# Delta-rule attention block: dense products regrouped behind the small ones, the next rows' norm moved to ScalarE

## The reference

```
q, k = l2norm(xn Wq) * 32**-0.5, l2norm(xn Wk)     16 heads of 32
v, beta = silu(xn Wv), sigmoid(xn Wb)
S_t = S_(t-1) + k_t (beta_t (v_t - S_(t-1)^T k_t))^T;  o_t = S_t^T q_t
attention = (rmsnorm(o) * o_norm_weight) Wo
FFN = ((silu(xn Wg * sg) * (xn Wu * su)) Wd) * sd   1536 inner, weights rounded to fp8
```

## Time and profile before

| | us |
|---|---|
| median of 3 runs | 2276.19 (2276.04 to 2282.8) |
| the profiled execution | 2288.38 |
| its span, first to last instruction | 2286.6 |
| TensorE busy with products | 2122.0 (93%) |
| VectorE busy | 1947.2 (85%) |
| ScalarE busy | 987.0 (43%) |
| GpSimd busy | 267.4 (12%) |

### The profile page before, as it was taken

How to read it: one execution, slowest core, us unless ns; L and a number is a source line. 1 busy time by engine, 2 the same in 40 slices (tenths; PEclk the granted TensorE clock), 3 DMA queues, 4 the chain that set the end, 5 groups by cost and what they waited for, 6 DMA issues and landing times.

```text
span 2286.6 us, 82010 instructions
## 1 busy us (share of the span) xinstructions
PE 2122.0 (93%) x36464; PEld 1089.5 (48%) x36592; DVE 1947.2 (85%) x3591; ACT 987.0 (43%) x2525; POOL 267.4 (12%) x519
## 2 busy tenths in 40 slices
PE   2889999999999999999999999999999999999996
PEld 1445454554545455454544545445444444445453
DVE  8988989889898988888878888887888878898886
ACT  4652534435353443535335353342534425354442
POOL 2101011020101102011010101101011020110200
PEclk9999999999999999999999999999999999999998
DMA  7001111001111100111100111001111001111000
GB/s 262 20 3 21 38 21 39 17 7 39 21 38 21 39 12 12 39 21 38 21 11 30 21 38 21 29 12 21 38 22 39 7 16 38 21 38 22 11 12 20
DMA packets 89951, 68.47 MB, mean 30 GB/s; under 512 B 68480, under 2 KB 68480, under 8 KB 89600
## 3 DMA queue, kind: packets, MB, share of 16 engines
q1 hardware_dynamic: 88880, 63.20, 9.7%
q10 hardware_dynamic: 720, 0.03, 0.0%
HBM read 30.72 MB, written 16.78 MB: 21 GB/s over the span
## 4 chain that ended last, share of the span: by engine, by line
PE 84%; DVE 10%; issue 4%; DMA 1%; ACT 0%; SPq 0%; DVEq 0%
PE D L456 25%; PE D L446 23%; PE D L519 13%; PE T L371 12%; PE D L387 7%; PE T L363 4%; DVE state L1386 1%; DVE f_lo L1218 1%; DVE stats L917 1%; DMA qt<-in_L_attn_Wq_dram 1%; DVE outer_v L1232 1%; DVE outer_p L1382 1%; DVE at L1239 1%; DVE at L920 0%; DVE kq L1254 0%
## 5 line engine op out<-in xcount | busy, mean ns | idle before, releaser
L456 PE MATMUL D<-xt,wgu 128*128 128x512 f16 x3072 | 689.4, 380 | 15.9 <-ACT sg L739 6.7
L446 PE MATMUL D<-xt,w_hi 128*128 128x512 f16 x1664 | 493.5, 383 | 26.0 <-DVE w_lo L1004 24.1
L456 PEld LDWEIGHTS D<-xt,wgu 128*128 128x128 f16 x3072 | 291.0, 98 | 365.0 <-issue 10.6
L519 PE MATMUL D<-wd,f_hi 128*128 128x512 bf16 x752 | 286.1, 380 | 17.8 <-issue 15.4
L446 PE MATMUL D<-xt,w_lo 128*128 128x512 f16 x768 | 294.5, 384 | 0.2 <-issue 0.2
L1232 DVE TENSOR_TENSOR outer_v<-mt,at 128x62 f32<-128x62 f32 (+15 forms) x496 | 260.2, 525 | 13.6
L1239 DVE TENSOR_TENSOR at<-at,outer_v 128x62 f32<-128x62 f32 (+15 forms) x496 | 260.9, 526 | 11.8
L446 PEld LDWEIGHTS D<-xt,w_hi 128*128 128x128 f16 x1664 | 160.1, 99 | 217.7 <-issue 33.9
L794 ACT ACTIVATE qt<-T 64x128 f32<-64x128 f32 (+1 forms) x384 | 104.7, 273 | 355.9 <-DVE outer_p L1382 352.9
L519 PE MATMUL D<-wd,f_lo 128*128 128x512 bf16 x656 | 248.6, 379 | 0.8
L729 ACT ACTIVATE kpv<-kpv,rk 128x32 f32<-128x32 f32 x1024 | 231.1, 308 | 35.1 <-DVE kpv L1096 35.1
(11 more groups left out here) (175 smaller groups left out, 2783.1 us busy)
## 6 DMA issues: line engine op xcount, KB each, us to landing
xs<-_attn_hidden_states_dram SPq DMA_DIRECT2D x32, 512.0 KB, 3.4
out_dram<-xs SPq DMA_DIRECT2D x32, 512.0 KB, 3.0
fuse<-in_L_ffn_gate_w_dram SPq DMA_DIRECT2D x2, 768.0 KB, 9.0
xs<-in_L_ffn_up_w_dram SPq DMA_DIRECT2D x2, 768.0 KB, 9.0
f_hi<-in_L_ffn_down_w_dram SPq DMA_DIRECT2D x2, 768.0 KB, 10.4
f_lo<-in_L_ffn_down_w_dram SPq DMA_DIRECT2D x2, 768.0 KB, 12.0
kpv<-in_L_attn_Wk_dram SPq DMA_DIRECT2D x1, 1024.0 KB, 11.5
qt<-in_L_attn_Wq_dram SPq DMA_DIRECT2D x1, 1024.0 KB, 13.7
```

The lines of the kernel that those rows point to most:

```text
L446: last = nc.tensor.matmul(D[bank][:, :], w[:, k, cols], xp[:, k, :], start=n == 0, stop=n == len(products) - 1)
L456: last = nc.tensor.matmul(D[bank][:, :], wgu[:, n // 2, c:c + P], (xt_hi, xt_lo)[n % 2][:, n // 2, :], start=n == 0, stop=n == 2 * KT_ - 1)
L519: last = nc.tensor.matmul(D[bank][:, :], (f_hi, f_lo)[n % 2][:, ic, j * P:(j + 1) * P], wd[:, ic, :], start=n == 0, stop=n == 2 * IC - 1)
```

## The change

Four things are moved; the arithmetic stays.

1. `FILL_UW` goes from 8 to 12, and `FILL_CHAIN` from 7 to (5, 7). 48 + 96 = 144 dense products as before: all six gate and up jobs now end before the chunk steps, and each down job takes exactly two steps.
2. `grams_of(1)` comes four dense products later, inside `project(6)`.
3. The next rows' norm is applied by ScalarE as an activation with scale `rstd` and bias `shift`, where VectorE makes `shift` = -mean * rstd for two tiles at once. The four tiles are spread over steps 1 to 4.
4. What follows from 1 is re-ordered: `silu_gate(11)`, `fuse_tile(10)`, `fuse_tile(11)`, `low_part(9)`, `high_part(11)` earlier, the squares of the queries in steps 2, 3, 5 and 6.

```diff
-HIGH_AT, LOW_AT = {1: (0, 1), 3: (2, 3)}, {2: 0, 3: 1, 4: 2, 5: 3}
-SQUARE_AT = {3: (0, 1), 4: (2, 3)}
+HIGH_AT, LOW_AT = {1: (0,), 2: (1,), 3: (2,), 4: (3,)}, {2: 0, 3: 1, 4: 2, 5: 3}
+SQUARE_AT = {2: (0,), 3: (1,), 5: (2,), 6: (3,)}
-APPLY_LATE = {0: 0, 2: 1}
+SHIFT_AT = {0: 0, 1: 1}
-FILL_UW, FILL_CHAIN = 8, 7
+FILL_UW, FILL_CHAIN = 12, (5, 7)
     # fill_at
-    return 4 * FILL_UW + (2 * c + half) * FILL_CHAIN
+    return 4 * FILL_UW + c * sum(FILL_CHAIN) + half * FILL_CHAIN[0]
     # TensorE
                     project(5)
+                    project(6, end=4)
                     grams_of(1)
-                    project(6)
+                    project(6, first=4)
-                        fill(fill_at(c, 0), FILL_CHAIN)
+                        fill(fill_at(c, 0), FILL_CHAIN[0])
-                        fill(fill_at(c, 1), FILL_CHAIN)
+                        fill(fill_at(c, 1), FILL_CHAIN[1])
     # ScalarE, before and in the chunk steps
                     silu_gate(10)
+                    silu_gate(11)
                         if c == 0:
                             high_part(10)
-                        if c == 1:
-                            silu_gate(11)
-                        if c == 2:
                             high_part(11)
+                        for j in () if closing else HIGH_AT.get(c, ()):
+                            act.wait_ge(shift_ready, since(BATCH, j // 2 + 1))
+                            act.wait_ge(tt_ready, since(2, 2))
+                            nc.scalar.activation(xn[:, j], xs[:, 1 - par, j, :], ACT.Identity, bias=shift[:, j:j + 1], scale=rstd[:, j:j + 1]).then_inc(xn_ready, 1)
     # VectorE
-                    def apply_norm(b):
+                    def shift_of(b):
                         if closing:
                             return
+                        two = slice(2 * b, 2 * b + 2)
                         dve.wait_ge(rstd_ready, since(BATCH, b + 2))
-                        dve.wait_ge(tt_ready, since(2, 2))
-                        for j in (2 * b, 2 * b + 1):
-                            layer_norm_apply(j, 1 - par).then_inc(xn_ready, 1)
+                        nc.vector.scalar_tensor_tensor(shift[:, two], mv[:, two, 0], -1.0, rstd[:, two], ALU.mult, ALU.mult).then_inc(shift_ready, 1)
                     read_w(7)
+                    fuse_tile(10)
                     low_part(8)
                     aggregate(0)
                     aggregate(1)
                         if c == 0:
-                            fuse_tile(10)
+                            fuse_tile(11)
                         if c == 1:
-                            low_part(9)
                             low_part(10)
-                        if c == 2:
                             low_part(11)
     # VectorE, after the state update of step c
-                        if c == 1:
-                            fuse_tile(11)
+                        if c == 0:
+                            low_part(9)
                         if c in LOW_AT:
                             low_x(LOW_AT[c])
-                        if c in APPLY_LATE:
-                            apply_norm(APPLY_LATE[c])
+                        if c in SHIFT_AT:
+                            shift_of(SHIFT_AT[c])
```

More of the change, by code:

```diff
@@ L154, in delta_block_kernel @@
         rstd = sb("rstd", [P, TILES])
+        shift = sb("shift", [P, TILES])
         ident = sb("ident", [P, P])
@@ L266, in delta_block_kernel @@
         v_step, p_step = sem("v_step"), sem("p_step")
-        q_out = sem("q_out")
+        q_out, shift_ready = sem("q_out"), sem("shift_ready")
         low_half, high_half = slice(0, P // 2), slice(P // 2, P)
```

## The result

| | before | after |
|---|---|---|
| median, us (4 executions each, side by side) | 2278.7 (2276.04 to 2282.8) | 2300.71 (2300.34 to 2301.35) |
| the profiled execution | 2288.38 | 2300.34 |
| its span | 2286.6 | 2298.6 |
| granted TensorE clock | 0.992 | 0.987 |

The ratio is 1.0095 (1.0076 to 1.0114): the kernel became slower by about 0.95%, 22 us. The forecast was 2292, within 2264 to 2311. The two profiled executions differ by less, 12.0 us of span. The kernel before varies more: 17 to 23 executions of it beside later experiments have medians of 2281.4 to 2282.2 and reach from 2274.7 to 2290.4, so that the 2276.19 from which the forecast counted lies at its low edge and the profiled 2288.38 at its high edge. Against 2282 the change costs 19 us.

A forecast was written before the change was run, and what follows sets the result against it. The prediction saw TensorE busy 93%, pausing for late instruction packets and ScalarE's last copy, with VectorE's loop losing its slack after the change. Pairs +19 and steps -3 gave +16: 2276.2 + 16 = 2292 us, range 2264 to 2311.

The forecast's parts named there:

- The stage of pairs: Inverse pairs up to the first state product: 17.32 us against a mean of 15.90 in ten turns; +19 us in all.
- The first and last turn: Pairs' stage some +2 us in each; in the chunk steps the closing turn gains some 2, the first 1.
- The chunk steps: Eight steps a turn: 37.8 us plus 0.9 of pauses, 38.7 against 38.73, nothing in 14 turns.
- Step 0: First chunk step: VectorE waits for `silu_gate(10)`, its transpose comes 1.7 us late, the step is 5.9 in place of 4.65.
- The edits at nothing: Norm on ScalarE, `shift_of`, SyncE's transfers and `silu_gate(11)`: no effect; bound for the norm 0 to 0.3 us a turn.
- step 3's old 0.7: Extra 0.7 us counted for step 3 in the old order's reckoning of 38.2 us a turn.
- The grams: `grams_of(1)` starts 0.86 us later, pauses in grams 2 and 3 stay: 0, bounds -24 and +4 us.
- Rule and row: Profile row: pauses inside sets are late instruction packets. Skill's rule: fetch hidden, pauses stay, sum higher by 21 us.
- Rival 3, the clock: TensorE's granted clock falls through step 0's wait in each turn: 14 x 1.6 = +22 us, 2313; chance 0.06.
- the frame: Profiled execution 2288.38 stands 12 us above the runs' median: 2304 profiled, median 2276.2 + 16 = 2292.

The follow-up runs named there:

- the repetition: The kernels before and after run and profiled once more, with empty instructions that the program that ran didn't hold: 2280.7 and 2300.0 us.
- step 0's order undone: The kernel after with `fuse_tile(10)` back behind step 0's subtraction and `fuse_tile(11)` behind its state update: 2275.22 us, 0.9972 of before.
- the halves swapped: The kernel after with seven dense products behind the state products and five behind the updates, `FILL_CHAIN` (7, 5): 2304.78 us, 1.0099 of before.
- the split after: The kernel after with one gate job a turn made as 16 products on 256 columns in place of 8 on 512: 2276.0 us, 0.9974 of before.
- the split kernel: The kernel before with one gate job a turn made as 16 products on 256 columns in place of 8 on 512: 2245.7 us, 0.9835 of before.

## Why the prediction was right, and where it was not

**The stage of pairs: right.** 3 x 4.22 + 1.53 + 3.13 = 17.32 was worked out; turns 1 to 9 have 17.30 to 17.40, and the small pauses inside the sets are gone in them, as supposed. The pause at the first sets stayed in turns 10 to 14, with 18.16 to 18.95, where the forecast left 18.8 in turns 10 to 13; these four add to 74.7 for 75.3. In 14 turns +15.7 for +15.2. The first and last turn were mis-sized: +3.8 as a whole for +1, and +7.6 in the repetition. Their pairs' stages alone took 6.3 and 6.2 more, for 4.

**The chunk steps: the mechanism right, the pauses mis-sized.** The steps of a quiet turn add to 37.76, forecast 37.8; before they add to 38.03, for 38.2. Step 0 is 5.95 to 6.04 for 5.9, with VectorE idle ahead of L1229 until ScalarE's L741 ends; step 1 4.62 for 4.63; steps 2 and 6 4.22; steps 3 and 5 4.83 for 4.83; step 4 4.41 for 4.43; step 7 4.59 for 4.73. The experiment with step 0's order undone shows the gate's wait by itself: 23 us. The forecast let the pauses grow from 0.55 a turn to 0.9, but they stayed at 0.7 (542.21 / 14 = 38.73 and 538.21 / 14 = 38.44), so that the stage gave back 4.0 where the forecast had 0.

**The edits at nothing: the sum right, the reason wrong.** The forecast put step 3's old 0.7 on GpSimd's addition, and said that the norm on VectorE lay mostly in slack. The norm alone on ScalarE takes 0.52 out of step 3, and GpSimd's part, which is left, is 0.18 beside a second half of seven; in the kernel after it is the whole 0.61 above 4.22, since the slack is gone. The norm left on VectorE would have cost 14.5 us there. The two terms had been added in one, so the sum stood. An activation of 512 columns with scale and bias took 0.80 to 0.81, forecast 0.65, and delayed nothing.

**The grams: right.** 0 was forecast. The -3.4 is the pause of turn 7, which the kernel before lacks in its second profile too; there the stage differs by -0.6. The instructions ahead of grams 2 and 3 are the same in number, and the pauses from turn 8 on stayed.

**Rule and row.** The forecast held the pauses to be the instruction supply, against the Trainium skill, "Runtime: NRT & Kernel Launch", section "Instruction fetch mechanics", which says that the fetch is hidden, the crossing of a block's boundary "mostly". The 84 gaps at one place of 256, their end 1.19 to 1.59 us behind a packet and the 36 us that 16 further instructions give decide for the row, in this kernel. A block of 256 instructions and the queue's 16.4 KB per packet fit the block size that this section states.

**Rival 3, the clock: in part.** In turns 4, 5 and 11 the granted clock is 0.96 over some 39.4 us, and each time the low stretch begins in step 0, behind TensorE's wait for VectorE: of the two levels some 3.4 us at 1.2 GHz. Step 0 is 6.84, 7.17 and 7.48 there. Steps 0 and 1 together are longer by 1.2 to 1.6 us in each, 4.5 in all, where the rival had 14 x 1.6. In the repetition of after it was turns 4, 11 and 12, with the norm back on VectorE four turns, and with the halves swapped and in the split after none, though step 0 is the same 6.04 there. What decides is open. The profiled execution has a mean granted clock of 0.987, the other three of after 0.980 to 0.981, so that in those it may be more turns.

**The median.** Counted from the profiled execution the forecast was 4 too high (2304 for 2300.34), counted from the median 9 too low (2292 for 2300.71). The step that failed is the frame: the three executions of before were low by 6 us as a set, and its profiled one was high by as much. That the sum of +16 lies so near is in part luck: in the repeated pair of profiles (+17.5) the first and last turn cost 6.6 more than forecast, and the steps and the grams gave back 5.4 that the forecast didn't have. The range was wide enough for either.

**What stays open.** Why the packet sets out 1.1 us after the boundary before in one set and 4.8 in another, which makes the pause 0.4 or 2.4 us long: the numbering explains where, the packet's start how long, and nothing here why it starts late. And what makes the executions of the kernel before differ by 16 us while those of after lie within 4 (2297.8 to 2301.8, nine of them with the repetition).

## What to carry to other kernels

Move filling work into a hole that the trace shows (behind the fourth set, -16 us), not behind each instruction of a kind: behind the other sets the same products cost 36 us, of which only pauses that went away gave back 20, and the steps from which they were taken were held by VectorE. Before an operation goes forward in an engine's queue, look for the last of its inputs in the trace and at what stands behind it; one multiplication ahead of its gate cost 25 us, more than the whole change lost. And where pauses have no semaphore, number the instructions: if they fall on one remainder, a handful of instructions more or fewer per turn is the cheapest edit there is. Then look where the boundary has come to stand instead.

## What the hardware showed that was not expected

- When TensorE pauses inside a set of small calls without a semaphore, it is at a place that recurs every 256 instructions: 84 gaps of 0.35 to 2.6 us in three kernels, all at the 195th or 196th instruction of 256 as they are counted here, and all ending 1.19 to 1.59 us after a packet of the instruction queue. Sixteen more instructions in a turn of 4594 made the kernel faster by 1.65%.
- Empty instructions given to TensorE were not in the traced program at all.
- The granted clock fell to the lower of its two levels for 3.4 us after TensorE had waited 1.7 to 1.8 us in step 0, in 3 turns of 14, and not in the other 11 with the same wait. In the kernel before it fell in the grams of turns 8 to 10, behind pauses of 2.1 to 2.4 us, but not behind those of 2.2 and 2.3 in turns 7 and 11, and with the split kernel in none of turns 1 to 14.
- A state update that takes 0.88 us alone takes 1.46 beside a GpSimd addition of 512 columns.
